# Routed experts: tiles of 128 places in place of 256, and each tile's expert weights loaded from DRAM by SyncE in place of copied on chip by VectorE

## The reference, cut to what matters

```python
x = x + _L1_ffn_ref(_layernorm(x)[None], Wg, bg, W1, b1, W2, b2)[0]

gate_scores = x @ Wg + bg                      # 4096 x 8
_, idx = top_k(gate_scores, 2)
mask = one_hot(idx, 8).sum(axis=-2)
h = gelu(einsum('td,edh->teh', x, W1) + b1)    # W1: 8 x 128 x 256
y = einsum('teh,ehd->ted', h, W2) + b2         # W2: 8 x 256 x 128
out = einsum('ted,te->td', y, mask)
```

## Time and profile before

| what | us |
|---|---|
| median of 3 runs | 892.39 (887.04 to 893.5) |
| profiled execution, its own time | 889.89 |
| its span, first to last instruction | 888.1 |
| of it before the first row load of the routed loop (SyncE, 712.5) | 712.5 |
| routed loop, first row load to the first load of `mixed` (867.3) | 154.7 |
| ending, from there | 20.9 |

### The profile page before, as it was taken

One profiled execution on the slowest core, in us unless ns is written; L12 is line 12 of the kernel. 1 busy time (PEld: TensorE's weight loads), 2 busy tenths in 40 slices (PEclk: granted clock), 3 DMA queues, 4 the chain that ended last, 5 costly groups with the idle time before them and its releaser, 6 DMA issues. The chain is left out here.

```text
span 888.1 us, 11394 instructions
## 1 busy us (share of the span) xinstructions
PE 721.2 (81%) x3372; PEld 422.0 (48%) x3372; DVE 587.4 (66%) x1691; ACT 471.3 (53%) x695; POOL 195.0 (22%) x233
## 2 busy tenths in 40 slices
PE   2748999999999999999729954699999865687840
PEld 1643444444444444444318843454454454576730
DVE  7785668787878788788757687645465662443424
ACT  1746888888888888888635451313113231222210
POOL 2240000000000000000006422003454347466660
PEclk9978999999999999999959986799999966799885
DMA  4108989998899998878240000300011032232218
GB/s 134 62 0 252 305 259 259 256 268 254 259 262 264 258 260 256 264 236 256 74 125 1 1 1 7 111 10 25 28 35 38 25 80 74 60 85 77 75 32 283
DMA packets 104620, 124.57 MB, mean 140 GB/s; under 512 B 9950, under 2 KB 82914, under 8 KB 104560
## 3 DMA queue, kind: packets, MB, share of 16 engines
q1 hardware_dynamic: 100016, 115.32, 45.3%
q0 software_dynamic: 4544, 8.54, 3.0%
HBM read 88.54 MB, written 36.20 MB: 140 GB/s over the span
## 5 line engine op out<-in xcount | busy, mean ns | idle before, releaser
L552 DVE SCALAR_TENSOR_TENSOR probs<-adj,probs 128x1024 f32<-128x1024 int32 x128 | 156.7, 1224 | 76.8 <-ACT probs L525 73.6
L475 PE MATMUL ps<-x,qT 128*128 128x512 f16 x768 | 188.8, 383 | 3.2 <-PEq L198 3.2
L525 ACT ACTIVATE probs<-ps 128x1024 f32<-128x1024 f32 x128 | 131.1, 1024 | 51.7 <-PE ps L475 51.7
L536 ACT ACTIVATE mask<-probs 128x1024 fp8e4<-128x1024 f32 x128 | 134.0, 1047 | 0.0
L487 PE MATMUL ps<-probs,v 128*128 128x512 f32 x256 | 130.7, 592 | 0.0
L1376 PE MATMUL ps<-mask,parts 128*128 128x512 fp8e4 x512 | 119.3, 389 | 7.4 <-DVE parts L1640 7.4
L475 PEld LDWEIGHTS ps<-x,qT 128*128 128x128 f16 x768 | 75.7, 99 | 95.4 <-issue 6.7
L1623 POOL DMA_INDIRECT mixed_spill<-mask,xn x78 | 76.1, 976 | 53.1 <-issue 27.7
L558 DVE TENSOR_TENSOR p_lo<-probs,p_hi 128x512 f16<-128x512 f32 x128 | 87.5, 684 | 0.1
L1550 ACT ACTIVATE mask<-ps,mask 128x256 f32<-128x256 f32 x78 | 32.5, 472 | 98.4 <-remote 45.9
L1576 POOL DMA_INDIRECT sorted_rows_spill<-rows,slots x64 | 63.1, 986 | 98.5 <-issue 54.1
(11 more groups left out here) (277 smaller groups left out, 969.8 us busy)
## 6 DMA issues: line engine op xcount, KB each, us to landing
adj<-in_adj SPq DMA_DIRECT2D x128, 512.0 KB, 5.0
sorted_rows_spill<-blank SPq DMA_DIRECT2D x32, 528.0 KB, 6.7
sorted_rows_spill<-blank SPq DMA_DIRECT2D x26, 198.0 KB, 7.5
xn<-sorted_rows_spill SPq DMA_DIRECT2D x39, 132.0 KB
mask<-mixed_spill SPq DMA_DIRECT2D x8, 512.0 KB, 5.9
mask<-in_x SPq DMA_DIRECT2D x4, 512.0 KB, 5.8
feat_spill<-mask SPq DMA_DIRECT2D x8, 256.0 KB
x_feat<-in_x SPq DMA_DIRECT2D x8, 256.0 KB, 5.1
```

The lines of the kernel that those rows point to most:

```text
L475: ins = nc.tensor.matmul(out, qT[:, q_half, j], kT[:, c, k_half * GROUP:(k_half + 1) * GROUP], start=(n == 0), stop=(n == 2))
L525: nc.scalar.activation(probs[:, k % RING, :], ps[:, b:b + 2, :].rearrange("p b n -> p (b n)"), ACT.Exp, scale=1.0 / QK_SCALE ** 2).then_in ...
L536: nc.scalar.activation(mask[:, k * W:(k + 1) * W], probs[:, k % RING, :], ACT.Sign, saturate=False).then_inc(mask_kept, 1)
L552: nc.vector.scalar_tensor_tensor(out=probs[:, k % RING, :], in0=adj[:, k % LOADS, :], scalar=0.0, in1=probs[:, k % RING, :], op0=ALU.is_gt ...
```

## The change

A tile has 128 places in place of 256, so there are 71 tiles, 41 of them early, and the loop's two side steps move to the tiles that lie at about the same rows (1, 1, 3, 4 and 16). The resident `weights` and the five DMAs that filled it are gone. The host lays each expert's W1, W2, b2 and b1 side by side in one DRAM tensor `Wb` of 8 x 128 x 642, and SyncE loads the tile's own 128x642 block into a ring of six sets, each with a semaphore of its own. For that it reads a second value (the expert) from the table. VectorE no longer reads the table or copies weights. Loads, products, gelus, outputs and scatters are of 128 places; a tile has one scatter.

```diff
-ROUTED_STEPS = (2 * N + E * (2 * P - 1)) // (2 * P)
+ROUTED_STEPS = (2 * N + E * (P - 1)) // P
-EARLY = -(-(2 * GROUP * EARLY_CHUNKS - E * (2 * P - 1)) // (2 * P))
+EARLY = -(-(2 * GROUP * EARLY_CHUNKS - E * (P - 1)) // P)
-MOST_TILES = N // (2 * P)
+MOST_TILES = N // P
-        WEIGHTS = 3
-        current = room.take(WEIGHTS, EXPERT_WIDTH)
-        tokens = room.take(RING, 2 * P)
-        hT = room.take(SLOTS, FH, 2 * P)
-        y = room.take(LOADS, 2, D)
+        WEIGHTS = 6
+        current = buf("current", [P, WEIGHTS, EXPERT_WIDTH])
+        tokens = room.take(RING, P)
+        hT = room.take(SLOTS, FH, P)
+        y = room.take(LOADS, D)
-        CHOOSE_AT, STAGE_AT, RANK_AT, SCATTER_AT, TABLE_AT = 0, 0, 1, 2, 8
+        CHOOSE_AT, STAGE_AT, RANK_AT, SCATTER_AT, TABLE_AT = 1, 1, 3, 4, 16
@@ SyncE: the five loads of the resident weights are gone, and in the loop over k
-                    start = sp.value_load(table[0:1, 1, k:k + 1], min_val=0, max_val=E * N + (ROUTED_STEPS - 1) * 2 * P)
+                    start = sp.value_load(table[0:1, 1, k:k + 1], min_val=0, max_val=E * N + (ROUTED_STEPS - 1) * P)
+                    one = bass.ds(sp.value_load(table[0:1, 0, k:k + 1], min_val=0, max_val=E - 1), 1)
                     if k >= LOADS:
-                        sp.wait_ge(y_out[u], 32 * (k // LOADS))
-                    sp.dma_start(sorted_rows[:, u, :, :], io["sorted"][bass.ds(start, 2 * P), :].rearrange("(h p) n -> p h n", p=P))\
-                        .then_inc(rows_in[u], 16)
+                        sp.wait_ge(y_out[u], 16 * (k // LOADS))
+                    sp.dma_start(sorted_rows[:, u, :], io["sorted"][bass.ds(start, P), :]).then_inc(rows_in[u], 16)
+                    if k >= WEIGHTS:
+                        sp.wait_ge(y_ready, k - WEIGHTS + 1)
+                    v = k % WEIGHTS
+                    sp.dma_start(current[:, v, :], io["Wb"][one, :, :].rearrange("a p n -> (a p) n")).then_inc(weights_in[v], 16)
@@ TensorE
-                    for h in range(2):
-                        ins = nc.tensor.transpose(ps[:, XT_BANK + k % 2, h * P:(h + 1) * P], sorted_rows[:, u, h, 0:D], sb["ident"][:, :])
-                    ins.then_inc(tile_turned, 1)
+                    nc.tensor.transpose(ps[:, XT_BANK + k % 2, 0:P], sorted_rows[:, u, 0:D], sb["ident"][:, :]).then_inc(tile_turned, 1)
-                    pe.wait_ge(current_ready, k + 1)
+                    pe.wait_ge(weights_in[k % WEIGHTS], 16 * (k // WEIGHTS + 1))
@@ ScalarE, in gelus(k); the same wait stands in keep_outputs(k) on VectorE
+                    act.wait_ge(weights_in[k % WEIGHTS], 16 * (k // WEIGHTS + 1))
@@ GpSimd
-                    for h in range(2):
-                        nc.gpsimd.indirect_dma_start(
...
-                            in_=y[:, u, h, :], in_offset=None, bounds_check=2 * N - 1, oob_is_err=False).then_inc(y_out[u], 16)
+                    nc.gpsimd.indirect_dma_start(
...
+                        in_=y[:, u, :], in_offset=None, bounds_check=2 * N - 1, oob_is_err=False).then_inc(y_out[u], 16)
@@ VectorE
-                def load_weights(k):
-                    e = dve.value_load(table[0:1, 0, k:k + 1], min_val=0, max_val=E - 1)
-                    if k >= WEIGHTS:
-                        dve.wait_ge(y_ready, k - WEIGHTS + 1)
-                        dve.wait_ge(down_ready, k - WEIGHTS + 1)
-                    nc.vector.tensor_copy(current[:, k % WEIGHTS, :], weights[:, bass.ds(e, 1), :].rearrange("p a n -> p (a n)"))\
-                        .then_inc(current_ready, 1)
```

More of the change, by code:

```diff
@@ L394, in attend @@
         BLANKS = E * N // (STEPS // 4)
-        TAIL_ROWS = 2 * P * ROUTED_STEPS
+        TAIL_ROWS = P * (ROUTED_STEPS + 1)
         TAIL = 3 * P
@@ L1119, in _ @@
                 ch.mark(nc.vector.tensor_scalar(place[:, :], place[:, :], float(N), None, ALU.mult))
-                ch.mark(nc.vector.tensor_scalar(sb["bound"][:, :], step[:, 0:MOST_TILES], float(2 * P), None, ALU.mult))
+                ch.mark(nc.vector.tensor_scalar(sb["bound"][:, :], step[:, 0:MOST_TILES], float(P), None, ALU.mult))
                 dve.wait_ge(gate_mean, 1)
@@ L1222, in gather_and_route @@
         ordered = buf("ordered", [P, E, E])
-        passed = buf("passed", [P, REST, E])
-        expert_of, first = buf("expert_of", [P, REST]), buf("first", [P, REST])
+        passed = buf("passed", [P, max(EARLY, REST), E])
+        expert_of, first = buf("expert_of", [P, max(EARLY, REST)]), buf("first", [P, max(EARLY, REST)])
         bound, used = sb["bound"], sb["used"]
-        table, weights = sb["table"], sb["weights"]
+        table = sb["table"]
         ROW_BANK, TURN_BANK, SMALL_BANK = 4, 6, 7
@@ L1289, in gather_and_route @@
         tokens_ready = sem("tokens_ready")
-        current_ready = sem("current_ready")
+        weights_in = [sem(f"weights_in{u}") for u in range(WEIGHTS)]
         up_ready = sem("up_ready3")
@@ L1318, in _ @@
             def _(sp):
[L1319 to L1324, removed]
                 count_ = sp.value_load(sb["levels"][0:1, 0:1], min_val=1, max_val=MOST_LEVELS)
@@ L1469, in down @@
                         pe.wait_ge(y_ready, k - 1)
-                    for h in range(2):
-                        for f in range(FH):
-                            ins = nc.tensor.matmul(ps[:, Y_BANK + k % 2, h * D:(h + 1) * D], hT[:, k % SLOTS, f, h * P:(h + 1) * P],
-                                                   current[:, k % WEIGHTS, F + f * D:F + (f + 1) * D], start=(f == 0), stop=(f == FH - 1))
+                    for f in range(FH):
+                        ins = nc.tensor.matmul(ps[:, Y_BANK + k % 2, 0:D], hT[:, k % SLOTS, f, :],
+                                               current[:, k % WEIGHTS, F + f * D:F + (f + 1) * D], start=(f == 0), stop=(f == FH - 1))
                     ins.then_inc(down_ready, 1)
@@ L1621, in _ @@
                     pool.wait_ge(y_ready, k + 1)
-                    for h in range(2):
-                        nc.gpsimd.indirect_dma_start(
-                            out=io["mixed"][:, :],
-                            out_offset=bass.IndirectOffsetOnAxis(ap=sorted_rows[:, u, h, D:D + 1].bitcast(U32), axis=0),
-                            in_=y[:, u, h, :], in_offset=None, bounds_check=2 * N - 1, oob_is_err=False).then_inc(y_out[u], 16)
+                    nc.gpsimd.indirect_dma_start(
+                        out=io["mixed"][:, :],
+                        out_offset=bass.IndirectOffsetOnAxis(ap=sorted_rows[:, u, D:D + 1].bitcast(U32), axis=0),
+                        in_=y[:, u, :], in_offset=None, bounds_check=2 * N - 1, oob_is_err=False).then_inc(y_out[u], 16)
             @block.vector
@@ L1721, in tile_starts @@
                         ch.link(nc.vector.tensor_scalar(first[:, 0:n], first[:, 0:n], at_, None, ALU.add))
-                    ch.link(nc.vector.scalar_tensor_tensor(out=first[:, 0:n], in0=step[:, 0:n], scalar=float(2 * P), in1=first[:, 0:n],
+                    ch.link(nc.vector.scalar_tensor_tensor(out=first[:, 0:n], in0=step[:, 0:n], scalar=float(P), in1=first[:, 0:n],
                                                            op0=ALU.mult, op1=ALU.add))
@@ L1869, in build @@
             with ExitStack() as rows:
-                for name, shape, dt in (("weights", [P, E, EXPERT_WIDTH], F32), ("table", [1, 2, ROUTED_STEPS], I32), ("e", [P, TILES], F32), ("valid", [P, TILES], F32), ("left", [P, 1], F32),
+                for name, shape, dt in (("table", [1, 2, ROUTED_STEPS], I32), ("e", [P, TILES], F32), ("valid", [P, TILES], F32), ("left", [P, 1], F32),
                                         ("levels", [P, 1], I32), ("xn", [P, TILES, D], F32),
@@ L1896 @@
         "Wg": L1_ffn_Wg, "bg": L1_ffn_bg,
-        "W1b": L1_ffn_W1, "b1b": np.asarray(L1_ffn_b1).reshape(E, FH, P).transpose(0, 2, 1), "W2b": L1_ffn_W2, "b2b": L1_ffn_b2,
+        "Wb": np.concatenate([np.asarray(L1_ffn_W1), np.asarray(L1_ffn_W2).reshape(E, FH, P, D).transpose(0, 2, 1, 3).reshape(E, P, FH * D),
+                              np.broadcast_to(np.asarray(L1_ffn_b2).reshape(E, 1, D), (E, P, D)),
+                              np.asarray(L1_ffn_b1).reshape(E, FH, P).transpose(0, 2, 1)], axis=2),
     }
```

29 lines of the change are left out of this document (12 added, 17 removed).

## The result

The changed kernel took 920.96 us on the median (919.17 to 923.64, four runs) against 892.94 (887.04 to 895.78, four runs) of the kernel before on the same chip. The ratio is 1.0326, interval 1.029 to 1.0362: **28 us slower**. The profiled execution took 923.64, its span is 921.9, and the mean granted clock 0.891.

What follows compares the result with a forecast made beforehand. SyncE's serial issue was taken to bind the changed loop: 750 + 59 tiles x 2.45 + 8.0 puts the load of mixed at 902.6 for 867.3, +35 us on 889.89, so 925, range 900 to 955.

Steps and rivals of the forecast that it cites:

- SyncE's serial need, 2.3 us a tile: Loop: SyncE's two table reads and two DMAs run one after another, 2.3 us a tile, above every other engine's need.
- Pace with lags, 2.45: Loop: SyncE's pace including waits the profile can't name, 2.45 us a tile over 59 tiles.
- Early table, +1.2: Ahead of the loop: the early table grows to 328 columns in four passes and 256 in two, +1.2 us.
- The block at tile 12 until 750: Loop: SyncE can't issue tile 12's rows until tile 4's scatter lands, about 750 us; costs 4 to 9 us.
- Tail, 8.0: End of loop: the last tile, from its weights' landing time through its last scatter's landing, takes 8.0 us.
- The sum: Whole loop: 750 + 59 tiles x 2.45 = 894.6, plus 8.0; mixed loaded at 902.6 for 867.3, +35 us.
- Traffic hidden, weights in 3.0 us: Loop: 23.3 MB of weights, 1.27 us of DMA time a tile, fits; one load lands in 3.0 us.
- VectorE's copies worth nothing: Loop: losing 39 VectorE copies, 20.0 us in all, gains nothing; VectorE's busy time falls some 25 us.
- Overlapping reads: Rival, 872: SyncE's second read and DMA overlap the first, so GpSimd binds at 1.28 us a tile; chance 0.11.
- More lags with more instructions: Rival, 948: unnamed waits follow all engines' instruction count, pace 2.8 us a tile, +56 us; chance 0.17.
- Late weights: Rival, 940: weight loads landing in over 10 us outlast six sets, about 2.7 us a tile; chance 0.05.
- The free GpSimd: Rival, 885: without VectorE's copies holding it up, GpSimd gains some 5 to 20 us in the loop; chance 0.01.

Runs made afterwards that it cites:

- the eleven buffers: Kernel after with eleven row and output buffers in place of eight: 898.75 us, ratio 1.0475 to the kernel before, 3.2 us less than the kernel after.
- a fifth of the bytes: Kernel after, each weight load bringing only 128 of 642 columns, the rest zeros set once: 904.11 us, ratio 1.0557 to the kernel before.
- 71 copies: Tiles of 128 with weights kept resident and copied by VectorE, SyncE issuing one read and one DMA a tile: 865.26 us, ratio 1.0091 to the kernel before.
- the fixed expert: Kernel after, tile k taking the weights of expert k mod 8, so one table read in place of two: 875.7 us, ratio 1.0212 to the kernel before.
- the two added reads: Kernel before with two more table reads a tile, values unused: 896.9 us against 894.69, ratio 1.0011.

## Why the prediction was right

The forecast, 925, came out at 921 by the likeliest case: SyncE's issue. By its own steps, in the profiled execution:

- **SyncE's serial need, 2.3 us a tile.** 2.17 measured, and a read less in each tile took its 0.6 us out of the period. The row load of 128 rows issues in 333 ns and not in the 382 of the load of 256, and so does the weight load; the reads cost what the row said. The Trainium skill, "Runtime: NRT & Kernel Launch", section "Instruction fetch mechanics", has about 200 ns a register for a TENSOR_LOAD; the trace shows 268 to 298 here too, and a check of 152 behind each.
- **Pace with lags, 2.45.** 2.27 measured. This is the term that was mis-sized, and 2.27 lies just under the 2.3 to 2.65 that had the chance of 0.60: 59 tiles at 2.45 are 144.6 us, from tile 12's rows to the last weights it took 132.4. Few lags fell on that stretch; without any it is 2.24.
- **Early table, +1.2.** 4.46 us from 711.11 to 715.57 against 3.34: +1.1. The first read stands at 715.8, 4.0 later than before; the other 2.9 us had come up in the gather, where this execution had more lags.
- **The block at tile 12 until 750.** 757.8, for another reason. The scatters of the last chunk ended at 750.6 and SyncE reached tile 12 behind them, held by a lag; the one wait of several us that was to show there isn't in this execution. On the chip without lags the block is there, 6.6 us of waits, and the eleven buffers price it at 3 us.
- **Tail, 8.0.** 10.4, from the last weights at 890.14 to `mixed` at 900.59. The last output starts 6.7 us behind that load where the steps forecast gave 4.75, since TensorE takes the last tile's up only at 894.26, behind the down of the tile before. From there to `mixed` it takes 3.7 in place of 3.24: the scatter of the tile before still runs.
```profile
896.87 0.29 DVE L1756 TENSOR_TENSOR mask<-ps,current 128x128 f32<-128x128 f32 x1 [0.57 <-PE ps L1467]
897.07 0.97 POOL L1618 DMA_INDIRECT mixed_spill<-mask,xn  x1 [0.51 <-issue]
898.34 0.97 POOL L1618 DMA_INDIRECT mixed_spill<-mask,xn  x1 [0.30 <-issue]
900.59 0.81 SPq L1349 DMA_DIRECT2D mask<-mixed_spill  x2
```
- **The sum.** +7.8 for the block, -12.2 for the pace, +2.4 for the tail: 902.6 became 900.6. The nearness of the result to 925 owes something to luck, errors of both signs; the mechanism doesn't. Two slips are in the recorded sums. The 925 is the profiled execution's time, and with the 2.5 us by which the median was said to stand higher it would be 927.5. The high end adds up to 890 + 59 + 2.5 = 951, not 955.
- **Traffic hidden, weights in 3.0 us.** 3.3 without lags, and a fifth of the bytes saved nothing.
- **VectorE's copies worth nothing.** Nearly. Taking away 39 of them, with a DMA in their place, won 4 to 5 us at tiles of 256, mostly as outputs that reach GpSimd earlier. "Nothing is there to get back" for the scatters was off by 15 ns: 987 with copies, 972 without, 1016 with 71 copies, about 1 us over 78. The Trainium skill, "SBUF — State Buffer", section "SBUF: two separate sides", has such copies lock GpSimd out of writing descriptors; the sign agrees, and the size here is 1.5% at tiles of 256 and 4.5% at tiles of 128 (1016 against the 972 of the fixed expert's run, on the same chip). VectorE's busy time fell by 8.4 us (587.4 to 579.0) and not by 25: outputs and turned rows now take 71 x 0.29 each where they took 39 x 0.42.
- **The rivals.** Overlapping reads fall by the trace, which has them in line, and by the fixed expert (0.59 us for one). More lags with more instructions fall by the two added reads for SyncE's, and for all engines' by the loop itself, which lost 10 us to lags after and 24 before. Late weights fall by the fifth of the bytes. The free GpSimd falls by the tiles of 256 with weights from DRAM, whose scatters were 15 ns shorter.

## What to carry to other kernels

Add up what one sequencer issues in one turn of the loop, register reads and checks included, and hold it against the slowest engine's time for the same turn: below it the issue is free (two added reads cost nothing), above it every step is paid in each tile, until another engine binds (26 us for one read, of the 0.6 x 71 = 43 that it takes). Halving a tile halves the work but not the issue, so a change that adds issue should be tried at the larger tile first. If a queue becomes the bound, moving part of it to another (20 us here) or dropping a read (26 us) wins time back.

## What the runs showed of the hardware

**Lags belong to the chip.** The kernel before took 893 to 895 us on two chips and 856 to 858 on three others. On the first two, single steps of SyncE are drawn out to 700 ns and releasers go unnamed ("remote"), and the gather ahead of the loop takes 138 to 142 us; on the traces of the others it takes 127 to 128, and in the loop nothing but the issue of a load takes over 0.6 us, at most four times. SyncE's issues at 721 to 730 of the kernel after, on the first chip; undisturbed they are 0.5 and 1.7 us apart by turns:
```profile
721.81 0.01 SPq L1337 DMA_DIRECT2D xn<-sorted_rows_spill  x1
...
723.24 0.01 SPq L1342 DMA_DIRECT2D current<-in_Wb  x1
...
728.96 0.01 SPq L1337 DMA_DIRECT2D xn<-sorted_rows_spill  x1
...
729.13 0.33 SPq L1342 DMA_DIRECT2D current<-in_Wb  x1
```
What makes them is open. With 78 more reads the unnamed waits didn't grow (43.6 us against 45.9).

**Landing under load.** A row load of 66 KB landed (median) in 1.9 us at 88 GB/s, in the run with a fifth of the bytes, in 2.9 at 207, in the kernel after on the chip without lags, and in 3.4 at 260, with the fixed expert, where the DMA share was 0.89.
